# Drains on GpSimd behind each row gather and each edge list gather of a graph attention and mixture-of-experts kernel

## What is computed

```python
feat_all = jnp.einsum('ni,rhid->rnhd', inputs, conv_weights)
feat_src_e = feat_all[edge_type, edge_src]
feat_dst_e = feat_all[edge_type, edge_dst]
el = jnp.sum(feat_src_e * attn_l[edge_type], axis=-1)
er = jnp.sum(feat_dst_e * attn_r[edge_type], axis=-1)
e = jax.nn.leaky_relu(el + er, negative_slope=LEAKY_SLOPE)
...
alpha = ex / denom[edge_dst]
h = jax.ops.segment_sum(alpha[..., None] * feat_src_e, edge_dst, num_segments=N_NODES)
...
x = x + _L0_gnn_ref(_layernorm(x, axis=-1), ...)
x = x + _L0_ffn_ref(_layernorm(x, axis=-1)[None], ...)[0]
```

## Time and profile before

| | |
|---|---|
| median of 3 runs | 2641.83 us |
| the profiled execution | 2645.0 us |
| its span | 2643.3 us |
| busy: TensorE, VectorE, ScalarE, GpSimd | 52%, 48%, 29%, 44% of the span |
| mean granted TensorE clock | 0.754 |
| software DMAs (GpSimd's queue) | 152.01 MB, 21.6% of 16 DMA engines |
| HBM read and written | 164.02 and 40.46 MB |

### The profile page before, as it was taken

The page is one execution under the profiler, slowest core; times in us unless marked ns, Lnnn a source line. Parts: engine busy times, 40 slices in busy tenths (PEclk is TensorE's granted clock), DMA queues, the critical chain, the costliest instruction groups (busy, mean ns, idle before and its releaser), DMA issues.

```text
span 2643.3 us, 26543 instructions
## 1 busy us (share of the span) xinstructions
PE 1373.6 (52%) x6717; PEld 1074.6 (41%) x6717; DVE 1264.1 (48%) x2568; ACT 772.2 (29%) x2841; POOL 1156.4 (44%) x1213
## 2 busy tenths in 40 slices
PE   6997300254554445544544555545454545454577
PEld 2443100143444334444434445444343444444465
DVE  5341134345654355553445555445444454555573
ACT  3542110122323123332212333233222323333351
POOL 0546275746434554343545434443444444444400
PEclk9999655577877678777667877777777777777798
DMA  4645752423222222122222222222222222222200
GB/s 119 194 147 151 226 165 71 108 59 91 61 55 61 79 76 68 55 62 56 74 70 75 64 56 62 65 64 56 61 65 64 62 62 62 60 62 62 62 5 3
DMA packets 85962, 206.12 MB, mean 78 GB/s; under 512 B 31329, under 2 KB 43214, under 8 KB 81784
## 3 DMA queue, kind: packets, MB, share of 16 engines
q0 software_dynamic: 57360, 152.01, 21.6%
q10 hardware_dynamic: 9452, 33.82, 4.1%
q1 hardware_dynamic: 18980, 18.80, 2.7%
HBM read 164.02 MB, written 40.46 MB: 77 GB/s over the span
## 4 chain that ended last, share of the span: by engine, by line
another core or an unknown queue 30%; PE 18%; issue 17%; DVE 13%; ACT 7%; DVEq 2%; ACTq 1%; DMA 0%; POOL 0%; POOLq 0%
PE y_ps L1450 10%; PE hid_ps L1436 7%; DVE fold_ps L1028 4%; ACT rows L1356 4%; DVE rows L1024 3%; ACT hT L1346 3%; DVE xo L1197 1%; DVE rden L1013 1%; DVEq L966 1%; DVE fold_ps L1024 0%; DVEq L53 0%; DMA node_row<-node_tab,idx_st 0%; DVE er_hot L981 0%; PE zt_ps L1460 0%
## 5 line engine op out<-in xcount | busy, mean ns | idle before, releaser
L878 POOL DMA_INDIRECT rows<-table,idx_st x1008 | 964.2, 957 | 556.1 <-issue 308.2
L1450 PE MATMUL y_ps<-w,hT 128*128 128x256 f32 (+1 forms) x1920 | 564.9, 452 | 667.6 <-ACT hT L1346 473.2
L1450 PEld LDWEIGHTS y_ps<-w,hT 128*128 128x128 f32 (+1 forms) x1920 | 413.4, 224 | 776.4 <-ACT hT L1346 490.3
L1436 PE MATMUL hid_ps<-zT,w 128*128 128x128 f32 (+1 forms) x3840 | 540.7, 296 | 321.0 <-issue 320.7
L1436 PEld LDWEIGHTS hid_ps<-zT,w 128*128 128x128 f32 x3840 | 516.4, 211 | 355.6 <-issue 343.9
L1346 ACT ACTIVATE hT<-hid_ps,b1t 128x128 f32<-128x128 f32 (+1 forms) x960 | 269.8, 366 | 1300.8 <-remote 1050.8
L1028 DVE TENSOR_TENSOR fold_ps<-rows,fold_ps 128x780 f32<-128x780 f32 (+1 forms) x348 | 326.2, 937 | 53.1 <-remote 31.5
L1356 ACT ACTIVATE rows<-rows,ex 128x65 f32<-128x65 f32 x1320 | 328.8, 349 | 30.3 <-issue 28.3
L886 POOL DMA_INDIRECT out_dram<-xo,oid x30 | 29.9, 995 | 569.5 <-DVE oid L1203 536.9
L1197 DVE SCALAR_TENSOR_TENSOR xo<-y_ps,cw,xo 128x256 f32<-128x256 f32 (+1 forms) x240 | 115.9, 483 | 271.6 <-PE y_ps L1450 192.0
L586 PE MATMUL feat_ps<-wc,xnT 128*125 128x512 f32 x480 | 222.3, 607 | 14.5 <-issue 12.3
(11 more groups left out here) (185 smaller groups left out, 916.2 us busy)
## 6 DMA issues: line engine op xcount, KB each, us to landing
table<-stage ACTq DMA_DIRECT2D x30, 924.0 KB
rows<-table,idx_st POOLq DMA_INDIRECT x1008
w<-in_L_ffn_W_dram SPq DMA_DIRECT2D x16, 512.0 KB
node_tab<-x_all SPq DMA_DIRECT2D x3, 1120.0 KB
table<-stage ACTq DMA_DIRECT2D x30, 107.2 KB
x_all<-in_x_dram SPq DMA_DIRECT2D x2, 1120.0 KB
wc<-_L_gnn_conv_weights_dram ACTq DMA_DIRECT2D x2, 1024.0 KB, 9.4
x_all<-in_x_dram SPq DMA_DIRECT2D x2, 560.0 KB
```

Source lines behind the costliest of these rows:

```text
L878: q.indirect_dma_start(buf[:, k, :], None, table, bass.IndirectOffsetOnAxis(idx[:, col + k:col + k + 1], 0)).then_inc(landed, 16)
L1436: last = t.matmul(hid_ps[e % 2][:, m * P:m * P + n], w1[:, e, k, m * P:(m + 1) * P], zT[:, k, 0:n], start=(k == 0), stop=(k == KD - 1))
L1450: last = t.matmul(y_ps[p % 2][0:n, (e % 2) * D:(e % 2 + 1) * D], hT[e % 2][:, k, 0:n], w2[:, e, k, :], start=(k == 0), stop=(k == KH - 1))
```

## The change

Two lines are added, both on GpSimd: a drain behind each edge list gather, and one behind each row gather of `gather`, which serves both `rows` and `xrows`. The gathers at lines 342, 895 and the scatters at lines 349 and 886 get none.

```diff
@@ phase1, gpsimd
                 g.indirect_dma_start(idx_all[:, w, :], None, edge_row.rearrange("(n o) -> n o", o=1),
                                      bass.IndirectOffsetOnAxis(rank_sb[:, w, 1:2].bitcast(U32), 0)
                                      ).then_inc(idx_in, 16)
+                pool.drain()
             pool.wait_ge(idx_in, 16 * W)
```

## The result

The kernel with the drains takes 4454.3 us, the median of 4 runs (4452.86 to 4459.13), beside 2639.68 us of the kernel before on the same chip (4 runs, 2637.15 to 2642.64). The ratio is 1.688, 95% interval 1.685 to 1.691. The profiled execution took 4452.86 us with a span of 4451.2. The forecast was 4370 us in a range of 3650 to 4900.

The account below looks back on a forecast made before the run. The kernel was taken as held by waits, its bursts of gathers holding up the other engines. First row gather 376, gathers 3664, per-window steps 210, one wait 21 and tail 95 gave 4366, rounded to 4370 us, range 3650 to 4900.

Parts of the forecast that it names:

- The pitch: Start to start of row gathers with a drain behind each: 3.55 us instead of 1.25, bounds 2.70 and 4.05.
- the last rival: A drain has its own cost beyond the landing: pitch 5.85 us, about 6800 us in all; chance 0.04.
- Phase 1: Edge list gathers at 3.85 us each, 115.5 instead of 42.9 us, partly covered; phase 1 ends 65 us later.
- GpSimd alone sets the window: Phase 2: 28 to 40 gathers take 99 to 142 us per window against 77 today; GpSimd waits for nobody.
- The sum: Whole kernel: 376 + 3664 + 210 + 21 + 95 = 4366 us, rounded to 4370.
- scatter to node rows 5.0 us: GpSimd's step between bursts in each window, part of 7.5 us per window, 210 us in 28 windows.
- The further batch: One wait of GpSimd for VectorE's fold of a further batch, 20.7 us.
- The tail: From the last rows' landing, at VectorE's last line 986, to the span's end: 95 us.
- The crawl: Other engines slow from about a burst's sixteenth gather until some 5 us after its end; would end or be covered.
- the drain waits for the instruction alone: Rival: a GpSimd drain ends once descriptors are written; pitch 1.8 us, about 2505 us in all; chance 0.06.
- its other form, in which the crawl stays: Rival: pitch 1.8 us, and each window still ends with its burst: 3230 us; chance 0.03.
- a drain is nearly free: Rival: a drain fits under the 0.30 us of issue or adds about 0.01 us per gather: 2656 us; chance 0.03.

Follow-up runs that it names:

- the wait in its place: Kernel before, no drains; GpSimd waits on each edge list gather's own landing semaphore: 2704.01 us, 53 more than before.
- the second drain of 53 ns: Two drains behind each row gather, none behind the edge list gathers: 4486.85 us, against 4382.02 with one drain each.
- the memset's 1.86 us: Kernel before, no drains; behind each of a window's first 28 row gathers GpSimd clears one spare column and waits for that: 2375.96 us, later 2378.7.

## Why the prediction was right, and where it was off

**The pitch: right, one of its two terms partly by luck.** 3.55 us was forecast as 2.78 for the landing and 0.77 for the next dispatch. The median from one row gather's start to the next is 3.56 us (978 such pairs, from the timeline), the mean 3.62: the first ones, beside the weight loads, are slow (388.02 to 394.89, 6.9 us). The page has 2.8 us from issue to landing. The reading that a drain looks after its DMAs stood on two rows, 2510 and 8067 ns; that it is the landing is shown by the wait in its place, the second drain of 53 ns, and the memset's 1.86 us. The 0.77 was taken from a GpSimd released from a wait, with no cost for the drain. But the edge list gather that waited for a landing of 2.5 us was followed by the next after 2.73 us, so the dispatch took 0.2 to 0.3 us, and a drain in the wait's place made it 3.19. So the 0.8 us behind a landing are some 0.25 of dispatch and some 0.5 that only the drain costs; they add up to the forecast's 0.77.

**A cost beyond the landing: far under the last rival's 2.3 us, but not tens of ns.** It was put down to "a small sum over many", which one drain per gather would pay in pieces of tens of ns. The end's drain shows the sum. Between the last drain before it and the end stand 4 indirect DMAs in the changed kernel, 4 in that with a drain at every fourth gather, 8 at every eighth, 16 with one per window:
```profile
L129 POOLq DRAIN  x1: 386/386/386, 2385.4 to 2385.4; - x1
```
```profile
L129 POOLq DRAIN  x1: 712/712/712, 2290.3 to 2290.3; - x1
```
```profile
L129 POOLq DRAIN  x1: 1366/1366/1366, 2502.8 to 2502.8; - x1
```
391 and 386 ns for 4, 712 for 8, 1366 for 16, 53 for none: close to 0.05 us and 0.08 for each. With 91 and 1092 undrained it is less for each (2510 and 8067 ns). For one DMA this gives 0.13 us of the 0.5 measured; where the other 0.3 to 0.4 go no run shows.

**Phase 1: right in sum, by two errors that cancel.** Phase 2's first row gather was forecast for 376 and came at 380.0, and phase 1 ended 69 us later (GpSimd's release from the barrier, 307.5 before and 376.9 now), not 65. The pitch of the edge list gathers was forecast as 3.85 us for all 30. In the trace it is 3.22 in the median (their landing takes 2.5 us, where the forecast had 3.07 from VectorE's start), which by itself would have given some 18 us less, and 3.92 in the mean, because the first few took up to 13.3 us. The prediction had named 20 us for those and left them out of its sum.

**GpSimd alone sets the window: right.** Its long waits for VectorE in the steady windows are gone, and VectorE waits for the rows for 2602 us.

**The sum: 4366 against a span of 4451.2, 85 short.** Phase 1 gives +4. From the first row gather to VectorE's last line 988 the sum had 3664 + 210 + 21 = 3895 us, the trace 4367.1 - 380.0 = 3987, 92 more. Of these 72 are the mean pitch of 3.62 in place of 3.55. The other term that was mis-sized is "scatter to node rows 5.0 us", read from one window: before the change the step takes 5.0 and 6.6 us in turn, with the drains 5.8 and 8.8 in turn, 7.4 in the mean of 25. The chain of waits shows two idle pieces in a long step (2083.10 to 2091.98), and only the first of them in a short one:
```profile
2084.53 2.70 issue
...
2087.37 2.87 issue
```
They lie between branches and register reads (lines 804, 772, 893); line 772, which stands on both sides of the second, is run in every second window, where the loop over pairs starts its next pass. In all 25 steps the queue named "instruction" (two queues have it, q14 here) moves packets just then: three in each of the 13 long steps, one in each of the 12 short ones (DMA view, from 1.3 us behind the scatter's start to 1.5 us ahead of the node rows), and only 4 in the 129 us of gathers that follow one. That fits a GpSimd that waits for its next instructions to be loaded, and no run varied it. Where GpSimd's program could run ahead the step took 1.30 us: in all 25 with one drain per window on the chip that doesn't crawl, against a mean of 7.4 with a drain behind each gather on the same chip. So its work is hidden under the gathers where the program has a lead, and laid open where it stands just before, at a wait for VectorE in the kernel before or at a drain. The further batch waited less (10.4 us, not 21). The tail is 84 us, not 95; 7.7 of the difference are the end's drain, 391 ns instead of 8067.

**The crawl: its effect right, its nature not known.** The prediction rested on the drained kernel's crawl ending or being covered, and it has none. It also said that "whatever changes a burst's pitch changes the window". That held in all runs, but for two reasons: on chips that crawl a slower pace or a pause can shorten the window, and on the one that doesn't the window is little else than GpSimd's gathers, so that each drain adds its price. Nothing in the trace of before could tell that on another chip the same program runs a burst with all engines busy.

**The rivals.** That the drain waits for the instruction alone falls: done by a memset, that pace gives 2376 us, and the change 4454. With it falls its other form, in which the crawl stays (3230 us). So falls the time of 2505 us that the prediction worked out by the rule of the Trainium skill's GPSIMD Engine Reference (Instruction dispatch). That rule is about when an instruction is complete; a drain waits for more. That a drain is nearly free falls as well (2656 by the Trainium skill's VectorE: DVE Perf Modes, The DRAIN you can't avoid). Its 12 ns are near the 7 that SyncE's shows, and GpSimd's took 53 ns with nothing issued since the last, 2678 at the least behind a row gather. The prediction called VectorE's rows near it as well; those of the earlier trace rows are 708 to 981 ns, and the two at the phases' ends took 17 and 193.

## What to carry to other kernels

A GpSimd drain behind an indirect DMA costs that DMA's full landing plus some 0.8 us; price it as the start-to-start pitch of DMAs, here 3.56 us against 1.25, and multiply by the count before anything else is considered. Where one landing has to be awaited, a wait on its semaphore does it for 0.4 to 0.5 us less. A drain also ends the program's lead over its engine, so what stands behind the last DMA of a burst has to be priced as laid open. Where DMAs must be closed, close them in batches: a drain adds 2.3 us to the pitch behind one, 2.7 behind eight. And a kernel whose engines crawl beside a burst for a releaser that no view names should be timed on a second chip before anything is tuned against the crawl.

## What was not expected of the hardware

- **The same program took 2639 to 2651 us in three sets of runs (on two chips at least) and 1868 us in the fourth, on another chip**, a factor of 1.41. The crawl goes with it: beside bursts of the same pitch TensorE has 7 matmuls in 19.5 us in the one case and 100 in 19 us in the other. The time with a drain behind each gather differs by less than 0.2% once the edge list's part is set off (4446.5 and 4454.3). Why one chip crawls and another doesn't was not found; no run could vary it. The chip without the crawl was used in one set of runs only, so the chip and the occasion aren't told apart, and the kernel before left no trace there.
- Slower gathers can be the faster kernel: on crawling chips a pitch of 1.86 us, or a pause of 2.7 us at each eighth gather, gives 10% and 13%.
- Between two back-to-back gathers there is room of 0.30 us of which a small memset takes 0.14 without moving the next gather.
